# Three attention steps of a fused decoder layer with an order of their own on every engine

## What is computed

```python
# linear attention, 32 heads of 8
qkv = relu(x @ Wqkv.T); vk = einsum(v_padded_with_1, k); y = (vk @ q)[..., :D] / (vk @ q)[..., D:]
x = layernorm(x + y @ Wproj.T + b)
# cross attention with a context, 16 heads of 16, rotary positions from integer coordinates
q = rope2d(fp16(x @ Wq.T)); k = rope2d(fp16(ctx @ Wk.T)); v = ctx @ Wv.T
x = layernorm(x + softmax(q k^T * scale) v @ Wo.T + bo)
# feed-forward with low-rank factors, rank 64, inner width 1024
x = layernorm(x + gelu(x @ U1 @ V1 + b1) @ U2 @ V2 + b2)
```

## Time and profile before

| what | value |
|---|---|
| median of 3 runs | 535.34 us (535.23 to 536.82) |
| profiled execution, device time | 537.56 us |
| its span in the trace | 535.8 us |
| TensorE busy | 498.2 us (93%), VectorE 400.5 (75%), ScalarE 312.7 (58%), GpSimd 344.5 (64%) |
| granted TensorE clock, mean | 0.974 of full |
| chain that ended last, by engine | PE 74%, issue 10%, DVE 6%, POOL 5%, ACT 3% |

### The profile page before, as it was taken

One profiled execution on the slowest core, in us unless ns is written; L12 is line 12 of the kernel. 1 busy time (PEld: TensorE's weight loads), 2 busy tenths in 40 slices (PEclk: granted clock), 3 DMA queues, 4 the chain that ended last, 5 costly groups with the idle time before them and its releaser, 6 DMA issues.

```text
span 535.8 us, 11400 instructions
## 1 busy us (share of the span) xinstructions
PE 498.2 (93%) x4044; PEld 336.6 (63%) x4044; DVE 400.5 (75%) x878; ACT 312.7 (58%) x457; POOL 344.5 (64%) x391
## 2 busy tenths in 40 slices
PE   6997799999999999999999999999978788999992
PEld 3885566677676767676777767777745333645451
DVE  6567877888888888888888888878887765545453
ACT  3543266665657574748475656666566577565650
POOL 6649245867777778686877777787676425342525
PEclk9899899999999999999999999999989789999997
DMA  8663203020402040213202220302000001133332
GB/s 268 143 117 91 73 12 86 11 65 11 104 13 83 16 100 24 74 38 81 85 13 49 69 85 11 100 16 65 11 24 22 16 21 60 69 107 112 125 108 108
DMA packets 29132, 36.01 MB, mean 67 GB/s; under 512 B 5721, under 2 KB 15321, under 8 KB 29081
## 3 DMA queue, kind: packets, MB, share of 16 engines
q1 hardware_dynamic: 28216, 34.37, 22.4%
q10 hardware_dynamic: 864, 0.95, 0.7%
HBM read 23.51 MB, written 8.65 MB: 60 GB/s over the span
## 4 chain that ended last, share of the span: by engine, by line
PE 74%; issue 10%; DVE 6%; POOL 5%; ACT 3%; DMA 1%; POOLq 1%; SPq 0%; ACTq 0%
PE FR L1223 22%; PE BK L1223 12%; PE BK L1401 11%; PE SC L1382 6%; PE SC L1350 6%; PE FR L1310 4%; PE FR L1302 3%; PE FR L1287 3%; PE FR L1427 2%; POOL rs L648 2%; POOL c_fm L653 2%; PE SC L1223 2%; DVE nmax L1038 2%; PE SC L1587 1%; ACT probs L756 1%
## 5 line engine op out<-in xcount | busy, mean ns | idle before, releaser
L1038 DVE TENSOR_REDUCE nmax<-SC 128x4 f32<-128x1024 f32 x128 | 155.8, 1218 | 27.3 <-PE SC L1350 24.9
L756 ACT ACTIVATE probs<-SC 128x1024 f32<-128x1024 f32 x128 | 130.9, 1026 | 57.5 <-PE SC L1382 57.4
L1401 PE MATMUL BK<-probs,v_aug 128*32 128x256 f32 x1024 | 70.7, 393 | 1.0 <-ACT probs L756 0.7
L1350 PE MATMUL SC<-k_blk,q_grp 48*128 48x512 f16 x256 | 50.3, 389 | 9.1 <-DVE nmax L1038 8.3
L1382 PE MATMUL SC<-q_grp,k_blk 64*128 64x256 f16 x512 | 50.8, 279 | 5.1 <-ACT probs L756 2.5
L852 ACT ACTIVATE probs<-SC,b_ff 128x512 f32<-128x512 f32 x64 | 38.9, 688 | 25.9 <-PE SC L1592 25.9
L1401 PEld LDWEIGHTS BK<-probs,v_aug 128*32 128x32 f32 x1024 | 26.8, 110 | 28.5 <-issue 12.1
L1382 PEld LDWEIGHTS SC<-q_grp,k_blk 64*128 64x128 f16 x512 | 20.0, 96 | 32.6 <-issue 15.1
L718 ACT ACTIVATE lin_fm_h<-FR 128x512 fp32r<-128x512 f32 x15 | 9.0, 597 | 45.3 <-PE FR L1310 45.3
L648 POOL TENSOR_TENSOR rs<-ve,minus_half 128x2 f32<-128x2 f32 x16 | 11.1, 692 | 35.9 <-DVE nm L1209 35.9
L529 POOL TENSOR_TENSOR att_fm_l<-att_raw,att_fm_h 128x512 fp32r<-128x512 f32 x16 | 20.6, 1287 | 20.3 <-ACT att_fm_h L731 20.3
(11 more groups left out here) (239 smaller groups left out, 1537.1 us busy)
## 6 DMA issues: line engine op xcount, KB each, us to landing
x_fm<-in_x_fm SPq DMA_DIRECT2D x16, 256.0 KB, 5.4
x_tm<-in_x_tm SPq DMA_DIRECT2D x16, 256.0 KB, 5.0
x_kept<-x2b SPq DMA_DIRECT2D x16, 256.0 KB, 2.1
x_tm<-x_kept SPq DMA_DIRECT2D x16, 256.0 KB, 2.7
out<-c_fm SPq DMA_DIRECT2D x16, 256.0 KB, 2.0
c_fm<-in_c_fm SPq DMA_DIRECT2D x15, 256.0 KB, 5.4
tables<-rope_tables SPq DMA_DIRECT2D x16, 128.0 KB
k_blk<-k_rope SPq DMA_DIRECT2D x128, 16.0 KB, 1.8
```

Source lines behind the costliest of these rows:

```text
L756: act.activation(probs[:, j % 4], (SC[j % 2] if b == LAST else SB)[:], ACT.Exp, scale=SCALE).then_inc(s_exp, 1)
L1038: dve.tensor_reduce(nmax[:, t, :, 2 * q:2 * q + 2], src[:].rearrange("p (s f) t -> p s f t", s=2), AX.X, ALU.max, negate=True).then_inc(s_ ...
L1350: mm = pe.matmul(out[:, 2 * s:2 * s + 2].rearrange("p h t -> p (h t)"), q_grp[n % NB][rows, q, t * P:(t + 1) * P], k_blk[n % NB][rows, q]. ...
L1401: mm = pe.matmul(BK[q // 2][HP * k:HP * (k + 1), (q % 2) * T:(q % 2 + 1) * T], v_aug[b % NB][:, t, HC * q + k], probs[:, j % 4, k], start= ...
```

## The change

The engines' loops over `step(b)` end with step 12. Steps 13 and 14 get lists of their own on TensorE and ScalarE (`step_13`, `step_14`), and written-out calls on VectorE and GpSimd; the last step's lists are reordered. `scores1` of the next image and `scores2` of the present one stand in turn, with other products between. Some work moves across step borders: `pv_pair(13, 2)` and `(13, 3)` to step 14, `(14, 2)` and `(14, 3)` to step 15, the value product `v2(15)` and `p_ff(11)` to step 14, `p_ff(12)` stays in 14, the adds `add2(12)` and `add2(13)` each to the step after. Late products go to other banks: `k2(15)` and `wo(12)` to BK0, `x1_t(15)`, `q2(15)`, `v2(15)`, `wo(13)` and `wo(14)` to FR1, `x2_t(11)` and `x2_t(12)` to BK1, `p_ff(11)` to `p_ff(13)` to FR0, and the transposed maxima of image 15 to BK0. The waits for free banks follow. SyncE's list is unchanged. The diff, in the file's order (GpSimd, ScalarE, VectorE, TensorE), with unchanged lines left out:

```diff
...
-shift_t16 = FR[0][:].bitcast(F16)[:, 0:T]
+shift_t16 = [bank[:].bitcast(F16)[:, 0:T] for bank in (FR[0], BK[0])]
...
-    for b in range(LAST):
+    for b in range(LAST - 2):
...
+    rstd1(LAST)
+    rope_k_cos(LAST)
+    norm2(LAST - 4)
+    att_scale(LAST - 3)
+    rope_k(LAST)
+    rope_q_cos(LAST)
+    att_lo(LAST - 3)
+    rope_q(LAST)
+    pool.wait_ge(s_shift, LAST)
+    residual2(LAST)
+    keep_x2(LAST - 4)
+    norm2(LAST - 3)
+    att_scale(LAST - 2)
+    keep_x2(LAST - 3)
+    att_lo(LAST - 2)
     norm2(LAST - 2)
     att_scale(LAST - 1)
     att_lo(LAST - 1)
...
     def ev_shift(b):
...
-        act.activation(q_grp[b % NB][TR + PR:P], shift_t16[TR + PR:P].unsqueeze(1).broadcast_to([PR, HC, T]),
+        act.activation(q_grp[b % NB][TR + PR:P], shift_t16[b == LAST][TR + PR:P].unsqueeze(1).broadcast_to([PR, HC, T]),
...
-    def ev_x2t(q):
+    def ev_x2t(q, src=FR[1]):
...
-        act.activation(x2_fm[:].rearrange("p c t -> p (c t)"), FR[1][:], ACT.Copy).then_inc(s_x2t_ev, 1)
-    def ev_p(q):
+        act.activation(x2_fm[:].rearrange("p c t -> p (c t)"), src[:], ACT.Copy).then_inc(s_x2t_ev, 1)
+    def ev_p(q, src=FR[1]):
...
-        act.activation(p_hi[R:P], FR[1][R:P, 0:T], ACT.Copy).then_inc(s_p_hi, 1)
-        act.activation(p_fm[0:R, q * T:(q + 1) * T], FR[1][0:R, 0:T], ACT.Copy).then_inc(s_p_hi, 1)
+        act.activation(p_hi[R:P], src[R:P, 0:T], ACT.Copy).then_inc(s_p_hi, 1)
+        act.activation(p_fm[0:R, q * T:(q + 1) * T], src[0:R, 0:T], ACT.Copy).then_inc(s_p_hi, 1)
...
+    def step_13():
+        ev_shift(LAST - 2)
+        exp_chunk(LAST - 3, 7)
+        exp_chunk(LAST - 2, 0)
+        ev_k2(LAST, BK[0])
+        exp_chunk(LAST - 2, 1)
+        norm1(LAST, 0)
+        norm1(LAST, 1)
+        exp_chunk(LAST - 2, 2)
+        ev_x1(LAST, FR[1])
+        exp_chunk(LAST - 2, 3)
+        ev_q2(LAST, FR[1])
+        exp_chunk(LAST - 2, 4)
+        ev_att(LAST - 3)
+        exp_chunk(LAST - 2, 5)
+        ev_x2t(LAST - 4, BK[1])
+        exp_chunk(LAST - 2, 6)
+        exp_chunk(LAST - 2, 7)
+    def step_14():
+        ev_shift(LAST - 1)
+        exp_chunk(LAST - 1, 0)
+        exp_chunk(LAST - 1, 1)
+        ev_p(LAST - 4, FR[0])
+        exp_chunk(LAST - 1, 2)
+        exp_chunk(LAST - 1, 3)
+        exp_chunk(LAST - 1, 4)
+        ev_x2t(LAST - 3, BK[1])
+        ev_v2(LAST, FR[1])
+        ev_att(LAST - 2)
+        exp_chunk(LAST - 1, 5)
+        ev_p(LAST - 3, FR[0])
+        exp_chunk(LAST - 1, 6)
     def last_step():
+        ev_shift(LAST)
         exp_chunk(LAST - 1, 7)
-        ev_shift(LAST)
-        exp_chunk(LAST, 0)
-        exp_chunk(LAST, 1)
+        for j in range(6):
+            exp_chunk(LAST, j)
+        ev_att(LAST - 1)
         ev_x2t(LAST - 2)
-        exp_chunk(LAST, 2)
-        exp_chunk(LAST, 3)
-        ev_p(LAST - 2)
-        exp_chunk(LAST, 4)
-        ev_att(LAST - 1)
-        exp_chunk(LAST, 5)
         exp_chunk(LAST, 6)
         exp_chunk(LAST, 7)
-    for b in range(LAST):
+    for b in range(LAST - 2):
...
+    step_13()
+    step_14()
...
+    ev_p(LAST - 2, FR[0])
...
-    def ev_p(p):
+    def ev_p(p, src=FR[1]):
...
-        dve.tensor_tensor(p_fm[R:P, p * T:(p + 1) * T], FR[1][R:P, 0:T], p_hi[R:P].bitcast(F32),
+        dve.tensor_tensor(p_fm[R:P, p * T:(p + 1) * T], src[R:P, 0:T], p_hi[R:P].bitcast(F32),
...
     def ev_shift(b):
...
-        dve.tensor_copy(q_grp[b % NB][PR:2 * PR], shift_t16[PR:2 * PR].unsqueeze(1).broadcast_to([PR, HC, T])
+        dve.tensor_copy(q_grp[b % NB][PR:2 * PR], shift_t16[b == LAST][PR:2 * PR].unsqueeze(1).broadcast_to([PR, HC, T])
...
-    for b in range(LAST):
+    for b in range(LAST - 2):
...
+    add1(LAST)
+    row_max(LAST - 1, 0)
+    ev_shift(LAST - 2)
+    stats1(LAST)
+    row_max(LAST - 1, 1)
+    stats2(LAST - 4)
+    row_max(LAST - 1, 2)
+    turn_pv(LAST - 3, 1)
+    row_max(LAST - 1, 3)
+    att_norm(LAST - 3)
+    ev_x1(LAST, FR[1])
+    k_halves(LAST)
+    row_max(LAST - 1, 4)
+    att_turn(LAST - 3)
+    row_max(LAST - 1, 5)
+    q_halves(LAST)
+    row_max(LAST - 1, 6)
+    turn_pv(LAST - 2, 0)
+    row_max(LAST - 1, 7)
+    shift(LAST - 1)
+    row_max(LAST, 0)
+    ev_shift(LAST - 1)
+    row_max(LAST, 1)
+    add2(LAST - 3, BK[0])
+    row_max(LAST, 2)
+    stats2(LAST - 3)
+    row_max(LAST, 3)
+    turn_pv(LAST - 2, 1)
+    row_max(LAST, 4)
+    att_norm(LAST - 2)
+    ev_p(LAST - 4, FR[0])
+    row_max(LAST, 5)
+    att_turn(LAST - 2)
+    row_max(LAST, 6)
+    turn_pv(LAST - 1, 0)
+    row_max(LAST, 7)
+    shift(LAST)
+    add2(LAST - 2, FR[1])
     ev_shift(LAST)
+    ev_p(LAST - 3, FR[0])
     stats2(LAST - 2)
+    raise_p(0)
     turn_pv(LAST - 1, 1)
     att_norm(LAST - 1)
-    raise_p(0)
     raise_p(1)
+    raise_p(2)
     att_turn(LAST - 1)
-    raise_p(2)
     raise_p(3)
-    ev_p(LAST - 2)
     raise_p(4)
     turn_pv(LAST, 0)
     raise_p(5)
+    add2(LAST - 1, FR[1])
+    ev_p(LAST - 2, FR[0])
     raise_p(6)
-    add2(LAST - 1, FR[0])
     turn_pv(LAST, 1)
     att_norm(LAST)
     stats2(LAST - 1)
...
-            pe.wait_ge(s_proj_ev, B)
+            pe.wait_ge(s_v2_ev, LAST)
...
     def v2(n, out=BK[0]):
-        if n >= 2:
+        if n == LAST:
+            pe.wait_ge(s_q2_ev, B)
+        elif n >= 2:
...
+        elif b < LAST:
+            pe.wait_ge(s_shift_ev, 2 * b)
...
-            pe.wait_ge(s_q2_ev, B)
+            pe.wait_ge(s_pvc_ev, LAST)
...
-            mm = pe.transpose(shift_t16[:, t * P:(t + 1) * P], shift16[:, t], ident16[:])
+            mm = pe.transpose(shift_t16[b == LAST][:, t * P:(t + 1) * P], shift16[:, t], ident16[:])
...
-            pe.wait_ge(s_v2_ev, min(b + 2, B))
+            pe.wait_ge(s_v2_ev, b + 2 if b < LAST - 2 else b + 1)
...
-            if b == LAST:
-                pe.wait_ge(s_pvc_ev, b)
-        if j == 4 and b < LAST:
+            if b == LAST - 2:
+                pe.wait_ge(s_k2_ev, B)
+            elif b == LAST - 1:
+                pe.wait_ge(s_wo_ev, LAST - 2)
+            elif b == LAST:
+                pe.wait_ge(s_shift_ev, 2 * B)
+        if j == 4 and b < LAST - 2:
...
+        elif j == 4 and b < LAST:
+            pe.wait_ge(s_x2t_ev, b - 1)
...
     def wo(p, out=BK[1]):
...
+        if p == LAST - 3:
+            pe.wait_ge(s_pvc_ev, LAST - 1)
+        elif p == LAST - 2:
+            pe.wait_ge(s_v2_ev, B)
+        elif p == LAST - 1:
+            pe.wait_ge(s_x2t_ev, LAST - 1)
...
-    def x2_t(q):
+    def x2_t(q, out=FR[1]):
...
-        if on(q + 4):
+        if q < LAST - 4:
...
+        elif q < LAST - 2:
+            pe.wait_ge(s_pvd_ev, q + 2)
...
-        turn(FR[1], x2_tm, s_x2t_mm)
-    def p_ff(q):
+        turn(out, x2_tm, s_x2t_mm)
+    def p_ff(q, out=FR[1]):
+        if q == LAST - 4:
+            pe.wait_ge(s_shift_ev, 2 * LAST)
+        elif LAST - 4 < q < LAST - 1:
+            pe.wait_ge(s_p_ev, q)
...
-            mm = pe.matmul(FR[1][:, 0:T], w_u1[:, c], x2_fm[:, c], start=(c == 0), stop=(c == CC - 1))
+            mm = pe.matmul(out[:, 0:T], w_u1[:, c], x2_fm[:, c], start=(c == 0), stop=(c == CC - 1))
...
+    def pv_pair(b, k):
+        pv(b, 2 * k)
+        pv(b, 2 * k + 1)
+    def step_13():
+        b, n1, n, p, q = LAST - 2, LAST - 1, LAST, LAST - 3, LAST - 4
+        scores2(p, 7)
+        scores1(n1, 0)
+        shift_t(b)
+        scores2(b, 0)
+        scores1(n1, 1)
+        k2(n, BK[0])
+        scores2(b, 1)
+        scores1(n1, 2)
+        pv_pair(p, 3)
+        scores2(b, 2)
+        scores1(n1, 3)
+        x1_t(n, FR[1])
+        pv_pair(b, 0)
+        scores2(b, 3)
+        scores1(n1, 4)
+        q2(n, FR[1])
+        scores1(n1, 5)
+        scores2(b, 4)
+        pv_pair(b, 1)
+        scores1(n1, 6)
+        scores2(b, 5)
+        x2_t(q, BK[1])
+        scores1(n1, 7)
+        scores2(b, 6)
+        wo(p, BK[0])
+        scores2(b, 7)
+    def step_14():
+        b, n1, p, q = LAST - 1, LAST, LAST - 2, LAST - 3
+        scores1(n1, 0)
+        shift_t(b)
+        pv_pair(p, 2)
+        scores1(n1, 1)
+        scores2(b, 0)
+        p_ff(q - 1, FR[0])
+        scores1(n1, 2)
+        scores2(b, 1)
+        pv_pair(p, 3)
+        scores1(n1, 3)
+        scores2(b, 2)
+        pv_pair(b, 0)
+        scores2(b, 3)
+        scores1(n1, 4)
+        v2(n1, FR[1])
+        scores1(n1, 5)
+        scores2(b, 4)
+        x2_t(q, BK[1])
+        pv_pair(b, 1)
+        scores1(n1, 6)
+        scores2(b, 5)
+        p_ff(q, FR[0])
+        scores1(n1, 7)
+        scores2(b, 6)
+        wo(p, FR[1])
     def last_step():
+        shift_t(LAST)
         scores2(LAST - 1, 7)
-        shift_t(LAST)
+        pv_pair(LAST - 1, 2)
         scores2(LAST, 0)
         scores2(LAST, 1)
-        pv(LAST - 1, 6)
-        pv(LAST - 1, 7)
+        pv_pair(LAST - 1, 3)
         scores2(LAST, 2)
+        scores2(LAST, 3)
+        pv_pair(LAST, 0)
+        scores2(LAST, 4)
         x2_t(LAST - 2)
-        scores2(LAST, 3)
-        pv(LAST, 0)
-        pv(LAST, 1)
-        p_ff(LAST - 2)
```

(19 more changed lines are left out.)

## The result

| | before | changed |
|---|---|---|
| median | 536.06 us (535.23 to 536.82, 4 runs) | 527.76 us (527.06 to 529.45, 4 runs) |
| ratio of the runs | | 0.9839, 95% interval 0.9806 to 0.9871 |
| profiled execution, span | 537.56, 535.8 us | 527.06, 525.3 us |
| granted clock, mean | 0.974 | 0.984 |

The kernel is 8.3 us faster (the interval allows 6.9 to 10.4). The forecast was 527.6, from 7.7 us gained and a median before of 535.34. Later in this study the changed kernel was timed again, on a chip where the kernel before had 536.85: 529.49 us, a ratio of 0.9841 (0.9808 to 0.9875).

What follows compares the result with a forecast made beforehand. Idleness and half-rate matmul in steps 13 to 15 (45.0 us of matmul in 57.3) were taken as the bound. Gains 1.9 + 4.0 + 2.1 - 0.3 = 7.7 us from 535.34 give 527.6, range 525.0 to 532.2.

Steps and rivals of the forecast that it cites:

- Sum and sign: Whole kernel: 7.7 us gained, from a median of 535.34 to 527.6; chance of faster 0.90.
- Step 13: Image 15's first scores start at 409.3 instead of 411.18, with one clock fall on the key product: 1.9 us gained.
- rival (a): Step 13 has no clock fall: its term is 3.3, the sum 9.1, the time 526.2 us; chance 0.17.
- Rival (b): Step 13's GpSimd chain to the queries comes no earlier: first term 0, time 529.5 us; chance 0.14.
- Step 14: VectorE's list runs without waits, 16.3 us from first score product to shift's end instead of 20.45: 4.0 us gained.
- Rival (c): Wo of image 13 comes late, blocking the shift transpose, shift copy and image 15's scores: 532.0 us; chance 0.09.
- Last step: Six exponentials run without a pause; shift to FFN takes 13.3 us against 15.46: 2.1 us gained, bounds 0 and 2.5.
- The FFN's head: Low-rank evacuation of image 13 comes about 1 us later against the first FFN product: 0.3 us lost, bounds 0 and 1.
- (d): Steps 13 to 15: waits eat all three gains, so no change, 535.3 us; chance 0.05.
- (e): Slower: clock falls at step 13's head and again in steps 14 and 15; 539.5 us at 30% more; chance 0.05.

Runs made afterwards that it cites:

- e3: Changed kernel with the two weighted sums of image 12 put into the two waits at the head of step 13; median 528.29 us.
- e10: Changed kernel with 15 and 6 matmuls that nobody reads put on TensorE in the two waits at the head of step 13; median 526.89 us.
- e12: Changed kernel with e10's unread matmuls and e11's mended FFN head together; median 525.00 us, ratio 0.9783 to the kernel before.
- e2: Changed kernel with the last step's lists put back as before; steps 13 and 14 and the banks stay new; median 531.58 us.
- e6: Changed kernel with VectorE's add and statistics of image 12 together ahead of the second maximum of step 14; median 531.60 us.
- e11: Changed kernel with the FFN's head filled by moved work and both halves of image 13's low-rank evacuation placed early; median 527.97 us.
- e9: The changed kernel timed once more, unmodified, on a chip where the kernel before had 536.85; median 529.49 us, ratio 0.9841.
- e1: Kernel before with the new order in the last step alone; median 536.19 us against 536.90, ratio 0.9998.
- e7: Changed kernel with Wo of image 13 in its old bank BK1 instead of FR1; median 529.03 us.
- e5: Changed kernel with GpSimd writing image 12's attention low part behind image 15's rotated queries, and Wo of image 12 moved to step 14; median 529.86 us.
- e4: e3 with GpSimd also splitting the context of image 15 ahead of the addition that keeps x2 of image 10; median 528.08 us.

## Why the prediction was right

**Sum and sign.** 7.7 us were forecast; the medians say 8.3 and, in the later comparison, 7.4. In the traces it is 9.17 with the short half-rate stretch and 22.18 + 20.45 + 15.46 - 20.39 - 16.39 - 12.93 = 8.38 with the long one. That 527.76 came within 0.2 us of 527.6 is partly luck: the median before rose by 0.7 us with a fourth run, and the gain was 0.6 larger.

**Step 13**, forecast 1.9: measured 2.60 and 1.79. The working named how the stretch begins: the key product at once behind the context's low part, matmul scarce ahead of it, and one clock fall on that product (at 392.6; forecast were 3 us before 395.7, which in this profile, 1.33 us ahead, is 391.4). How it ends was read wrongly: this is the step of the working that failed. The forecast let the chain run through the normalisation of image 15 to its queries, with a GpSimd that is free when they come, 14.5 us behind the first mark. They were there at 13.9 (401.57 - 387.67), and GpSimd took them up 0.8 us later, at 402.34, since it was still rotating the keys:

```profile
400.97 0.60 ACT L727 ACTIVATE q<-FR 128x512 f16<-128x512 f32 x1 [0.95 <-PE FR L1317]
```

So GpSimd's own list sets the end of the queries. It starts behind the key product, has one wait over 0.2 us in it, for the reciprocals of image 12 (1.06 us at 398.74), and then runs to 407.15. The end of the queries less the end of the key product and less this wait is 12.1 to 12.2 us in all seven profiles with these lists and in e3, e10 and e12, though the wait goes from 0.20 to 1.46 us. The wait for ScalarE's attention copy, for which the forecast took 409.3 instead of 408.7, didn't come. This also says what a fall costs. In the first profile it lay on half of the key product and on the pair behind it, for which those reciprocals wait. In e2, e6 and e11, with the same lists, it lay on all of the key product, which ended 7.0 us behind the first mark as forecast, but not on the pair: the list began 0.7 us later, the wait shrank (0.30 us in e2), and the step was as long, 19.45 to 19.62 us. In e9 it lay on both, with a wait of 1.15 us, and the step took 20.39, where the forecast has 409.3 - 389.0 = 20.3. The 1.79 us gained there match the 1.9 by luck: that fall is twice as long as the forecast's, and the path behind it another one. The case without a fall was priced at 3.3 us for this step; with the unread matmuls the step gained 22.18 - 18.42 = 3.76. So rival (a) was a real state, but the kernel as changed was not in it in any profile. Rival (b) is out: the queries' chain came earlier by 2.6 us (1.8 in e9).

**Step 14**, forecast 16.3 us: measured 16.40 in every run with its order. Counting VectorE's list was the right way, since VectorE never waited there in the profile after; e6 shows the condition it rests on, that another item stands between two maxima. Rival (c) didn't come: the low part for Wo of image 13 ended at 422.00, 1.65 us ahead of the shift's end (1.6 forecast), the product ran from 422.15, and the shift transpose followed at 423.71.

**Last step**, forecast 13.3 us: measured 12.94. The first exponential of image 15 came 426.0 - 423.65 = 2.4 us behind the shift, not 2.57, and the tail behind the sixth took 4.9 instead of 5.0, since in the rows part of the low-rank product and Wo overlap. These are sizes, each under 0.3 us; together they put the gain, 2.52, at the upper bound of 2.5. The forecast had no word for the fall that lay in this step before and didn't come after, which may be 0.9 of it or somewhat more.

**The FFN's head**, forecast 0.3 lost: measured 0. The x2 transpose did wait, 0.25 us, but the wait ahead of the low-rank product shrank from 0.89 to 0.58, so ScalarE's activations still set that place. In e1, e6 and e7 the FFN took 0.55 to 0.7 us more, with one clock fall in the head in each (in e1, 449.5 to 453 at 0.52); this was not in the forecast.

**Rivals (d) and (e)** said that waits would eat the gains, or more clock falls in steps 14 and 15. The denser order had no fall there (1.00 in both) and no such waits. But e5, with Wo gone from the end of step 13, had a fall at the start of step 14, and that step was 1.8 us longer, in part by it: the mechanism of (e) is real and near.

## What to carry to other kernels

Where one engine's list is nearly full and another engine feeds it through a single buffer, count the list and put one other item between every two that need the buffer: the stretch then takes the list's own time, here 16.40 us against 15.8 of work. Cut a tail that is out of steady state by marks and compare lengths between marks; whole runs of one kernel differed by up to 4.8 us where such a length repeated within 0.05. Where such lengths differ, look at the clock in them first, and compare a run with one whose fall is as long. Look for stretches in which TensorE has only scattered matmuls: what is lost is not only the wait but the half-rate products behind it, and filling such waits with unread matmuls was worth 1.2 to 2.0 us in the traces here.

## What was not expected of the hardware

The place and the length of a clock fall differ between runs of one kernel: 3.4 us in one profile and 6.8 in another at the head of step 13, with 0.8 us between the two lengths of the step. Removing a wait ahead of it (e4) moved the fall, and with a product taken out of the end of the step (e5) a second one came; both cost more than they gave.

VectorE's clamp of 32 values per partition took 1.18 us at 406.00 and 0.18 at 423.03:

```profile
423.03 0.18 DVE L1096 TENSOR_SCALAR nmax_c<-nmax 128x32 f32<-128x32 f32 x1
```

The slow one began 0.01 us behind GpSimd's last addition (405.99, 1.16 us) and ended 0.03 us behind it. The statistics' small scalar operation took 0.81 us at 390.91, beside the context split, and 0.17 at 394.07. The Trainium skill (SBUF — State Buffer, "Who interferes with whom") describes an exclusive port pair that VectorE and GpSimd share and that such operations can take; the trace agrees, with 1.0 and 0.6 us lost on VectorE's list in step 13, which is busy for 18.05 of its 19.58 us. No run took both collisions away alone, so what they cost the whole is not known.
